# The scale and shift of every layer norm on ScalarE instead of VectorE, in a fused two-layer decoder

## The chip, the cores and the metric

The kernel runs on one core of a Trainium2 chip. The metric is device time in microseconds (us) of one execution. The core has five engines that work side by side, each on its own queue of instructions in a fixed order: TensorE (PE in the profile, with its weight loads as PEld), VectorE (DVE), ScalarE (ACT), GpSimd (POOL) and SyncE (SP, which here only issues transfers). They wait for one another with semaphores. An engine that waits holds up everything that stands behind the wait in its queue.

## The reference, cut to what matters

The input x has 16 sequences of 512 positions and 256 features. It goes through two decoder layers of three blocks each, and every block adds to x what it computes from a layer norm of x, so there are six layer norms:

```python
def _layernorm(x, axis=-1, eps=1e-05):
    m = jnp.mean(x, axis=axis, keepdims=True)
    v = jnp.var(x, axis=axis, keepdims=True)
    return (x - m) / jnp.sqrt(v + eps)
...
    x = x + _L0_attn_ref(_layernorm(x, axis=-1), ...)    # gated linear scan, with an RMS norm of its own
    x = x + _L0_xattn_ref(_layernorm(x, axis=-1), ...)   # cross attention, 16 heads, 64 keys
    x = x + _L0_ffn_ref(_layernorm(x, axis=-1), ...)     # linear with a low-rank term
    x = x + _L1_attn_ref(_layernorm(x, axis=-1), ...)    # LSTM of 20 cells that places Gaussian windows
    x = x + _L1_xattn_ref(_layernorm(x, axis=-1), ...)   # cross attention with a gate
    x = x + _L1_ffn_ref(_layernorm(x, axis=-1), ...)     # 8 experts, one chosen per row
```

All is computed in float32.

## The kernel before

**Units.** The 512 positions are cut into 4 chunks of 128 and the 16 sequences into 4 groups of 4. A unit is one chunk of one group in one layer: a tile `l_xres` of 128 partitions (positions) by 4 sequences by 256 features. There are 16 units of layer 0 and 16 of layer 1. Two units are in work at a time, in two lanes with tiles of their own (`l0_...` and `l1_...`; the profile leaves the number out). A third stream is the LSTM, which is a chain of 512 small steps over all 16 sequences.

**Stages.** Stage 0 has two loop bodies, each with two layer-0 units, one per lane. Stage 1 has two bodies, two layer-0 units and 64 LSTM steps in each. Stages 2 and 3 have four bodies each: a layer-0 unit in lane 0, a layer-1 unit in lane 1, and 32 LSTM steps. Stage 4 has four bodies with a layer-1 unit and 32 LSTM steps, and stage 5 four bodies with a layer-1 unit alone. In the trace the stages begin near 95, 230 (second body), 352, 722, 1450, 2153 and 2720 us.

**The norm.** A layer-0 unit has four norms (k = 0 to 3: before the scan, the attention, the linear block, and the one whose output feeds layer 1), a layer-1 unit two (k = 4 and 5). That makes 16 x 4 + 16 x 2 = 96 norms. One norm goes as follows. VectorE takes statistics (`bn_stats`, `bn_aggr`) of the two halves of the tile, two sequences each (step `stat`), and adds epsilon (L1034). GpSimd raises the variance to the power -1/2 (step `root`, L1332; `ln_rstd`). VectorE then makes `l_xnat`, (x - mean) x rstd, in four instructions of 128x256, two to a half (step `norm`, function `normalise`, L1050). TensorE transposes each half of `l_xnat` (step `turn`, L681), ScalarE copies both halves to `l_xT` (step `land`, L890) once the second `turn` is done, and the matmuls of the block follow. Norm k = 0 has a second root for the RMS norm (L1329), and its scale is the product of the two roots (`ln_tmp`, L1130).

**What sets the order.** Each stage body has a plan. `norm_steps`, `attention_steps`, `layer0_steps`, `layer1_steps` and `lstm_steps` list steps with an engine, an assumed cost and the steps that they need; `planned` places them one by one, by the earliest start and the longest rest of the way, and every engine's queue follows that order. Where TensorE would stand idle for long in stages 0, 4 and 5, `planned` also places matmuls on a constant (`warm`, L761) as fill. So a step that changes engine or cost changes the order of all five queues.

Other lines that the text names: L879 and L882 are the LSTM's two tanh on ScalarE, L1276, L1278, L1282 and L1288 its work on VectorE, and L753 its matmul. L1346, L1353 and L1358 are GpSimd's work in the attention, L1303 its addition of a bias row.

## Time and profile before

| | |
|---|---|
| median of 3 runs | 3200.73 us (3198.63 to 3203.84) |
| span of the profiled execution, first to last instruction | 3192.7 us |
| TensorE matmul busy | 2765.4 us (87%) |
| VectorE busy | 2130.4 us (67%) |
| ScalarE busy | 960.5 us (30%) |
| GpSimd busy | 1047.5 us (33%) |
| mean granted TensorE clock | 0.902 of full speed |

The span leaves out what comes before the first and after the last instruction; the median of the runs is 8.0 us above it. Busy shares are averages over stages that are limited by different things, so the rows further down are taken stretch by stretch: 95 to 352 us is stage 0, 352 to 722 stage 1, 722 to 2153 stages 2 and 3, and 2153 to the end stages 4 and 5.

### The profile page before, as it was taken

To read this page: it belongs to the slowest core of one execution; us is meant where nothing else is said; L and a number is where in the kernel's file an instruction comes from. 1 tells how busy PE (TensorE), PEld (TensorE's weight loads), DVE (VectorE), ACT (ScalarE), POOL (GpSimd) and SP (SyncE) were. 2 spreads that over 40 slices of the span, in tenths; PEclk is the share of its full clock that TensorE was granted. 3 is DMA by queue.
4 is the path that set the end of the run, shared out by engine and by line. 5 is a ranking of instruction groups with operands and counts; after the bars stand their busy time and mean duration, and the time that the engine had idled before them with its cause. 6 is when DMAs were issued, how large, how long until landed. Compare 5 with 4: busy or idle time off the path is not lost.

```text
span 3192.7 us, 37478 instructions
## 1 busy us (share of the span) xinstructions
PE 2765.4 (87%) x11655; PEld 1627.7 (51%) x11733; DVE 2130.4 (67%) x5978; ACT 960.5 (30%) x2361; POOL 1047.5 (33%) x956
## 2 busy tenths in 40 slices
PE   5799885976888889897988988898989899899999
PEld 2466453452545545464645555564555445555555
DVE  3576786877778687867778686866475655534434
ACT  0133242332323333332323233332222232222222
POOL 0264332233424242523425242513141321413422
PEclk9899996987898889888889898898989898999999
DMA  4210101011010100101010101001011010110100
GB/s 171 62 53 10 61 11 37 1 51 33 15 50 14 51 14 20 37 25 46 25 46 14 57 14 37 14 29 32 21 40 33 14 33 14 40 53 14 53 27 7
DMA packets 127163, 110.35 MB, mean 35 GB/s; under 512 B 31234, under 2 KB 126039, under 8 KB 126624
## 3 DMA queue, kind: packets, MB, share of 16 engines
q1 hardware_dynamic: 127008, 108.55, 11.0%
q8 instruction: 64, 1.05, 0.1%
q14 instruction: 91, 0.75, 0.1%
HBM read 76.81 MB, written 31.72 MB: 34 GB/s over the span
## 4 chain that ended last, share of the span: by engine, by line
PE 37%; issue 27%; DVE 24%; POOL 7%; ACT 2%; SPq 1%; DMA 1%; DVEq 0%; POOLq 0%; ACTq 0%
PE p L781 5%; PE p L687 4%; PE p L842 4%; PE p L720 4%; PE p L744 3%; PE p L854 3%; DVE l_xnat L1050 3%; DVE uprod L1276 3%; PE p L681 2%; PE p L698 2%; DVE l_scratch L1076 2%; PE pg L753 2%; DVE gates L1278 2%; PE p L734 2%; POOL l_scratch L1358 2%
## 5 line engine op out<-in xcount | busy, mean ns | idle before, releaser
L1346 POOL TENSOR_TENSOR l_kbd<-l_kg,headmask 128x512 f32<-128x512 f32 x256 | 265.5, 1047 | 388.4 <-PE p L720 289.7
L1332 POOL TENSOR_TENSOR ln_rstd<-ln_ve,neghalf 128x4 f32<-128x4 f32 x96 | 98.2, 1023 | 893.8 <-DVE ln_ve L1034 893.2
L744 PEld LDWEIGHTS p<-l_vg,l_scratch 128*128 128x128 f32 x2048 | 286.8, 215 | 122.0 <-DVE l_xnat L1093 64.7
L1353 POOL TENSOR_TENSOR l_scratch<-l_scratch,l_mx 128x512 f32<-128x512 f32 x256 | 266.9, 1046 | 200.0 <-DVE l_mx L1080 199.3
L744 PE MATMUL p<-l_vg,l_scratch 128*128 128x34 f32 x2048 | 297.2, 296 | 40.5 <-DVE l_xnat L1093 32.8
L720 PE MATMUL p<-l_kbd,l_qT 128*128 128x512 f32 x512 | 294.4, 666 | 40.9 <-DVE l_scratch L1076 40.9
L1276 DVE SCALAR_TENSOR_TENSOR uprod<-gates 16x40 f32<-16x40 f32 x512 | 187.0, 365 | 213.0 <-ACT gates L879 210.5
L879 ACT ACTIVATE gates<-pg 16x80 f32<-16x80 f32 x512 | 114.8, 224 | 700.8 <-PE pg L753 699.8
L761 PE MATMUL p<-warm 128*128 128x512 bf16 x1009 | 278.3, 399 | 5.9 <-issue 3.6
L842 PE MATMUL p<-l_xT,wfc 128*128 128x512 f32 x512 | 278.9, 637 | 1.1 <-DVE hr L1233 1.0
L681 PE MATMUL p<-ident,l_xnat 128*128 128x128 f32 x1024 | 195.2, 325 | 90.7 <-DVE l_xnat L1050 89.1
L854 PE MATMUL p<-wpj,hq 128*128 128x256 f32 x1024 | 264.9, 387 | 8.3 <-ACT hq L955 8.3
L753 PE MATMUL pg<-wcat,slots 128*16 128x80 f32 x1024 | 172.9, 255 | 112.3 <-DVE slots L1288 110.1
L753 PEld LDWEIGHTS pg<-wcat,slots 128*16 128x16 f32 x1024 | 58.4, 97 | 357.4 <-DVE slots L1288 193.2
L882 ACT ACTIVATE tcell<-gates 16x20 f32<-16x20 f32 x512 | 110.4, 216 | 432.1 <-DVE gates L1278 431.6
L854 PEld LDWEIGHTS p<-wpj,hq 128*128 128x128 f32 x1024 | 187.0, 190 | 90.9 <-issue 59.2
L681 PEld LDWEIGHTS p<-ident,l_xnat 128*128 128x128 f32 x1024 | 141.0, 167 | 168.9 <-DVE l_xnat L1050 131.5
L1076 DVE TENSOR_TENSOR l_scratch<-p,l_neg 128x512 f32<-128x512 f32 x256 | 174.2, 682 | 55.7 <-PE p L720 50.4
L734 PE MATMUL p<-ident,l_scratch 128*128 128x128 f32 x1024 | 181.4, 309 | 18.3 <-DVE l_xnat L1093 8.6
L908 ACT ACTIVATE l_scratch<-p 128x512 f32<-128x512 f32 x256 | 149.1, 589 | 146.6 <-PE p L734 145.9
L1278 DVE SCALAR_TENSOR_TENSOR gates<-uprod 16x20 f32<-16x20 f32 x512 | 175.2, 342 | 17.6
L1282 DVE SCALAR_TENSOR_TENSOR hnew<-gates,tcell 16x20 f32<-16x20 f32 x512 | 137.8, 269 | 73.1 <-ACT tcell L882 72.3
(165 smaller groups left out, 4764.6 us busy)
## 6 DMA issues: line engine op xcount, KB each, us to landing
xln<-xln_dram SPq DMA_DIRECT2D x40, 512.0 KB, 4.4
l_vg<-v_dram SPq DMA_DIRECT2D x32, 544.0 KB, 3.9
l_kg<-k_dram SPq DMA_DIRECT2D x32, 256.0 KB, 4.2
xln_dram<-l_xnat SPq DMA_DIRECT2D x16, 512.0 KB, 3.0
x_dram<-l_xres SPq DMA_DIRECT2D x16, 512.0 KB, 4.1
l_xres<-x_dram SPq DMA_DIRECT2D x16, 512.0 KB, 3.6
out<-l_xres SPq DMA_DIRECT2D x16, 512.0 KB, 2.9
xin<-in_x SPq DMA_DIRECT2D x12, 512.0 KB, 3.8
```

Source lines behind the costliest of these rows:

```text
L681: i = pe.transpose(banks[l][m][:, b * P:(b + 1) * P], src[:, b, m * P:(m + 1) * P], ident[:, :])
L720: pe.matmul(banks[l][j], w.qT[:, j, b * P:(b + 1) * P], w.kbd[b % 2][:, j, :, :].rearrange("p a k -> p (a k)"), start=True, stop=True).the ...
L734: i = pe.transpose(t_bank[l][:, p * P:(p + 1) * P], src, ident[:, :])
L744: i = pe.matmul(o_bank[l][:, q * VW:(q + 1) * VW], w.exT[:, j, p, :], w.vg[:, b, q * VW:(q + 1) * VW], start=True, stop=True)
L753: pe.matmul(pg[0:B, 0:80], slots[:, s % STEPS, :], wcat[:, :], start=True, stop=True).then_inc(l_pe, 1)
L761: pe.matmul(pg[:, :] if layer == 0 else banks[0][0], warm[:, 0:P], warm[:, :], start=True, stop=True)
L842: i = pe.matmul(banks[1][2 + i_ % 2], wfc[:, k, i_ * P:(i_ + 1) * P], tiles[1].xT[:, k, :], start=(k == 0), stop=(k == NH - 1))
L854: i = pe.matmul(pairs[1][:, b * D:(b + 1) * D], hq[i_ % 2][:, b * P:(b + 1) * P], wpj[:, i_, :], start=(i_ == 0 and b % 2 == 0), stop=(i_ ...
L1276: dve.scalar_tensor_tensor(uprod[:, :], gates[:, 0:40], 1.0, gates[:, 60:100], ALU.add, ALU.mult).then_inc(l_u, 1)
L1278: dve.scalar_tensor_tensor(gates[:, 80:100], uprod[:, 20:40], 0.5, uprod[:, 0:20], ALU.mult, ALU.add).then_inc(l_c, 1)
L1346: pool.tensor_tensor(w.kbd[b % 2][:, j, :, :], w.kg[:, j, b:b + 1, :].broadcast_to([P, NE, SK]), headmask[:, :].rearrange("p (a o) -> p a ...
L1353: pool.tensor_tensor(ex, ex, w.mx[:, i_ % 4, :].rearrange("p (a o) -> p a o", o=1).broadcast_to([P, NE, SK]), ALU.subtract).then_inc(t.shi ...
```

## The change

The step `norm` becomes two steps. A new VectorE step `offset` makes `shift` = -mean x scale for the four sequences at once, one instruction of 128x4. Then `norm` runs on ScalarE: four activations of the identity function, 128x256 each, with `scale` and `shift` as operands that hold one value per partition. The waits that stood ahead of the old step (for the root; for k = 0 also for the store of the former `l_xnat` and for its `turn`) are split between the two. A new wait on GpSimd keeps the first root of a layer-0 unit from overwriting `rstd` while the ScalarE still reads it for the unit before. In `norm_steps` the costs are 0.2 (0.4 for k = 0) for `offset` and 0.8 for each half of `norm`, where 0.65 stood.

```diff
--- before.py
+++ after.py
@@ -75,7 +75,9 @@
         self.stats, self.mv = sb(f"{name}_stats", [P, GB, 6]), sb(f"{name}_mv", [P, GB, 2])
         self.ve, self.rstd = sb(f"{name}_ve", [P, 2, GB]), sb(f"{name}_rstd", [P, 2, GB])
         self.tmp = sb(f"{name}_tmp", [P, 4, GB])
+        self.shift = sb(f"{name}_shift", [P, GB])
         self.small, self.inv, self.normed = sem(f"{name}_small"), sem(f"{name}_inv"), sem(f"{name}_normed")
+        self.offset = sem(f"{name}_offset")
         self.turned, self.landed = sem(f"{name}_turned"), sem(f"{name}_landed")
 
     def before(self, layer, n, k):
@@ -152,7 +154,8 @@
     steps += [("pool", "root", k, 1.0, [("stat", 2 * k + 1)])]
     if rms:
         steps += [("dve", "rms", 0, 0.6, [("root", k)]), ("pool", "root", 9, 1.0, [("rms", 0)])]
-    steps += [("dve", "norm", 2 * k + h, 0.65, [("root", 9 if rms else k)]) for h in range(2)]
+    steps += [("dve", "offset", k, 0.4 if rms else 0.2, [("root", 9 if rms else k)])]
+    steps += [("act", "norm", 2 * k + h, 0.8, [("offset", k)]) for h in range(2)]
     steps += [("pe", "turn", 2 * k + h, 0.45, [("norm", 2 * k + h)]) for h in range(2)]
     steps += [("act", "land", 2 * k + h, 0.5, [("turn", 2 * k + 1)]) for h in range(2)]
     return steps
@@ -883,7 +886,20 @@
 
             def act_step(lane, layer, family, i_, c, g, n, m):
                 t, w, l0 = at[lane], tiles[lane], scans[lane]
-                if family == "land":
+                if family == "norm":
+                    k, h = divmod(i_, 2)
+                    s = ln[lane]
+                    if h == 0:
+                        act.wait_ge(s.offset, s.before(layer, n, k) + 1)
+                        if k == 0 and positive(n):
+                            act.wait_ge(l0.xln_store, 16 * n)
+                            act.wait_ge(s.turned, 2 * s.before(0, n, 0))
+                    src, scale = (w.xres, s.rstd[:, 0, :]) if k else (xin[lane], s.tmp[:, 1, :])
+                    for b in (2 * h, 2 * h + 1):
+                        i = act.activation(w.xnat[:, b, :], src[:, b, :], ACT.Identity, bias=s.shift[:, b:b + 1],
+                                           scale=scale[:, b:b + 1])
+                    i.then_inc(s.normed, 1)
+                elif family == "land":
                     k, h = divmod(i_, 2)
                     if h == 0:
                         act.wait_ge(ln[lane].turned, 2 * ln[lane].before(layer, n, k) + 2)
@@ -1045,11 +1061,9 @@
                 dve.tensor_tensor(s.tmp[:, 2, :], s.mv[:, :, 0], s.rstd[:, 0, :], ALU.mult).then_inc(s.small, 1)
                 dve.tensor_scalar(s.tmp[:, 0, :], s.rstd[:, 0, :], 1.0, None, ALU.add).then_inc(s.small, 1)
 
-            def normalise(s, h, scale, src, dst):
-                for b in (2 * h, 2 * h + 1):
-                    i = dve.tensor_scalar(dst[:, b, :], src[:, b, :], s.mv[:, b, 0:1], scale[:, b:b + 1],
-                                          ALU.subtract, ALU.mult)
-                i.then_inc(s.normed, 1)
+            def offset(s, scale):
+
+                dve.scalar_tensor_tensor(s.shift[:, :], s.mv[:, :, 0], -1.0, scale, ALU.mult, ALU.mult).then_inc(s.offset, 1)
 
             def add_product(l, h, done):
 
@@ -1118,21 +1132,15 @@
                         statistics(s, h, small, w.xres)
                 elif family == "rms":
                     rms(s, s.before_small(0, n, 0), s.before_roots(0, n, 0))
-                elif family == "norm":
-                    k, h = divmod(i_, 2)
-                    if k:
-                        if h == 0:
-                            dve.wait_ge(s.inv, s.before_roots(layer, n, k) + 1)
-                        normalise(s, h, s.rstd[:, 0, :], w.xres, w.xnat)
+                elif family == "offset":
+                    if i_:
+                        dve.wait_ge(s.inv, s.before_roots(layer, n, i_) + 1)
+                        offset(s, s.rstd[:, 0, :])
                         return
-                    if h == 0:
-                        dve.wait_ge(s.inv, s.before_roots(0, n, 0) + 2)
-                        dve.tensor_tensor(s.tmp[:, 1, :], s.rstd[:, 0, :], s.rstd[:, 1, :], ALU.mult).then_inc(s.small, 1)
-                        if positive(n):
-                            dve.wait_ge(l0.xln_store, 16 * n)
-                            dve.wait_ge(s.turned, 2 * s.before(0, n, 0))
-                        dve.wait_ge(s.small, s.before_small(0, n, 0) + 11)
-                    normalise(s, h, s.tmp[:, 1, :], xin[lane], w.xnat)
+                    dve.wait_ge(s.inv, s.before_roots(0, n, 0) + 2)
+                    dve.tensor_tensor(s.tmp[:, 1, :], s.rstd[:, 0, :], s.rstd[:, 1, :], ALU.mult).then_inc(s.small, 1)
+                    dve.wait_ge(s.small, s.before_small(0, n, 0) + 11)
+                    offset(s, s.tmp[:, 1, :])
                 elif family == "base":
                     if i_ == 0:
                         if positive(n):
@@ -1328,6 +1336,8 @@
                         pool.wait_ge(s.small, s.before_small(0, n, 0) + 8)
                         pool.tensor_tensor(s.rstd[:, 1, :], s.ve[:, 1, :], neghalf[:, :], ALU.pow).then_inc(s.inv, 1)
                     else:
+                        if i_ == 0 and positive(n):
+                            pool.wait_ge(s.normed, 2 * s.before(0, n, 0))
                         pool.wait_ge(s.small, s.before_small(layer, n, i_) + 5)
                         pool.tensor_tensor(s.rstd[:, 0, :], s.ve[:, 0, :], neghalf[:, :], ALU.pow).then_inc(s.inv, 1)
                 elif family == "brow":
```

The plans come out in another order. Three places follow, in the names of the instructions: `l1_` and `ln1_` are tiles of lane 1, `p1` its PSUM banks.

VectorE, stage 5, loop body, around the first norm (k = 4). Before:

```order
L1251 TENSOR_SCALAR l1_scratch<-p1 1x512
L1252 ISA
L1253 TENSOR_TENSOR l1_scratch<-l1_scratch,jrow 1x512
L1254 REGISTER_ALU
L1255 TENSOR_TENSOR l1_scratch<-l1_scratch 1x4x128
L1125 REGISTER_ALU
L1050 TENSOR_SCALAR l1_xnat<-l1_xres,ln1_mv,ln1_rstd 128x256 x4
L1257 REGISTER_ALU
L1258 SCALAR_TENSOR_TENSOR l1_scratch<-l1_scratch 1x516
L1261 TENSOR_SCALAR l1_scratch<-l1_scratch 1x512
```

And now:

```order
L1259 TENSOR_SCALAR l1_scratch<-p1 1x512
L1260 ISA
L1261 TENSOR_TENSOR l1_scratch<-l1_scratch,jrow 1x512
L1262 REGISTER_ALU
L1263 TENSOR_TENSOR l1_scratch<-l1_scratch 1x4x128
L1137 REGISTER_ALU
L1066 SCALAR_TENSOR_TENSOR ln1_shift<-ln1_mv,ln1_rstd 128x4
L1265 REGISTER_ALU
L1266 SCALAR_TENSOR_TENSOR l1_scratch<-l1_scratch 1x516
L1269 TENSOR_SCALAR l1_scratch<-l1_scratch 1x512
```

The four instructions of the norm are gone from the middle of the `rows` work (the 1x512 instructions, for the next unit), and one of 128x4 stands in their place.

ScalarE, stage 5, loop body, around the second norm (k = 5), which follows the end of the attention. Before:

```order
L908 ACTIVATE l1_scratch<-p1 128x512 x3
L894 ACTIVATE l1_xT<-p1 128x512 x2
L889 ISA
L890 ACTIVATE l1_xT<-p1 128x512 x2
```

And now:

```order
L924 ACTIVATE l1_scratch<-p1 128x512 x4
L910 ACTIVATE l1_xT<-p1 128x512 x2
L893 REGISTER_ALU
L899 ACTIVATE l1_xnat<-l1_xres,ln1_shift,ln1_rstd 128x256 x4
L905 ISA
L906 ACTIVATE l1_xT<-p1 128x512 x2
```

Four activations now stand between the last copy of the attention (`l1_xT` by L894, L910 in the changed file) and the copy after the `turn` (L890, now L906).

ScalarE, stage 3, loop body, at the norm k = 0 of lane 0 between LSTM steps. Before:

```order
L879 ACTIVATE gates<-pg 16x80
L882 ACTIVATE tcell<-gates 16x20
L889 ISA
L890 ACTIVATE l0_xT<-p0 128x512 x2
L878 REGISTER_ALU
L879 ACTIVATE gates<-pg 16x80
L882 ACTIVATE tcell<-gates 16x20
L930 REGISTER_ALU
L931 ACTIVATE l1_scratch<-p1 1x512
```

And now:

```order
L882 ACTIVATE gates<-pg 16x80
L885 ACTIVATE tcell<-gates 16x20
L893 ISA
L895 REGISTER_ALU
L896 REGISTER_ALU
L899 ACTIVATE l0_xnat<-xin,ln0_shift,ln0_tmp 128x256 x4
L881 REGISTER_ALU
L882 ACTIVATE gates<-pg 16x80
L905 REGISTER_ALU
L906 ACTIVATE l0_xT<-p0 128x512
L885 ACTIVATE tcell<-gates 16x20
```

Between the two tanh of one LSTM step (`tcell`) and the first tanh of the next (`gates`) stood two copies of 128x512; now four activations stand there and one copy behind the tanh.

The number of `warm` matmuls grows from 70 to 82 in each body of stage 0, from 135 to 139 (134 to 135 in the last body) in stage 4, and from 135 to 141 (133 to 136 in the last) in stage 5: 24 + 13 + 21 = 58 more in all.

## Rows read from the trace of the kernel before

**Rows 1.** Page, parts 1 and 4: busy time of the engines; the chain's shares.

```profile
PE 2765.4 (87%) x11655; PEld 1627.7 (51%) x11733; DVE 2130.4 (67%) x5978; ACT 960.5 (30%) x2361; POOL 1047.5 (33%) x956
...
PE 37%; issue 27%; DVE 24%; POOL 7%; ACT 2%; SPq 1%; DMA 1%; DVEq 0%; POOLq 0%; ACTq 0%
```

**Rows 2.** Four stretches; columns PE, PEld, DVE, ACT, POOL busy, then clock, DMA.

```profile
95.00:352.00 257.00, 238.15 (x1080) 150.98 (x1090) 174.29 (x489) 80.64 (x140) 114.59 (x98) 0.97 0.14 41
352.00:722.00 370.00, 292.53 (x1219) 164.25 (x1220) 290.63 (x987) 126.73 (x384) 119.60 (x111) 0.86 0.09 27
722.00:2153.00 1431.00, 1227.70 (x4980) 742.82 (x4979) 1090.37 (x2956) 466.65 (x1170) 516.46 (x468) 0.87 0.10 30
2153.00:3192.70 1039.70, 953.15 (x4060) 541.49 (x4126) 542.09 (x1442) 279.79 (x658) 296.67 (x276) 0.94 0.10 29
```

**Rows 3.** The chain by line, of 352 to 722 and of 722 to 2153.

```profile
by line: PE p L781 12.8%; PE p L687 10.4%; DVE uprod L1276 6.0%; PE pg L753 6.0%; PE p L720 5.3%; DVE l_xnat L1050 5.2%; DVE gates L1278 5.1%; issue 4.4%; PE p L744 4.3%; DVE hnew L1282 4.2%; PE p L698 3.4%; DVE slots L1288 3.3%; DVE ln_sta
...
by line: issue 17.1%; PE p L687 5.5%; PE p L842 4.9%; PE p L744 4.8%; PE p L854 4.7%; DVE uprod L1276 4.5%; PE p L720 4.1%; PE p L781 3.8%; DVE l_scratch L1076 3.8%; DVE l_xnat L1050 3.7%; PE p L681 3.4%; DVE l_mx L1080 2.7%; DVE gates L127
```

**Rows 4.** Line L1050 alone in the four stretches: its busy time on DVE.

```profile
95.00:352.00 257.00, 26.56 (x64) 0.97 0.14 41
352.00:722.00 370.00, 28.30 (x64) 0.86 0.09 27
722.00:2153.00 1431.00, 102.68 (x192) 0.87 0.10 30
2153.00:3192.70 1039.70, 35.32 (x64) 0.94 0.10 29
```

**Rows 5.** Waits of the turns for L1050, stretch by stretch: total, times, longest.

```profile
PE p L681 <- DVE l_xnat L1050: 19.6, 11, 13.3
...
PE p L681 <- DVE l_xnat L1050: 10.7, 8, 2.9
...
PE p L681 <- DVE l_xnat L1050: 36.0, 25, 3.7
...
PE p L681 <- DVE l_xnat L1050: 22.9, 16, 2.6
```

**Rows 6.** Groups by shape: busy us, mean ns of one; line L1050's min/median/max.

```profile
L882 ACT ACTIVATE tcell<-gates 16x20 f32<-16x20 f32 x512 | 110.4, 216 | 432.1 <-DVE gates L1278 431.6
...
L903 ACT ACTIVATE l_scratch<-l_scratch 128x512 f32<-128x512 f32 x256 | 158.4, 620 | 65.1 <-POOL l_scratch L1353 64.6
...
L908 ACT ACTIVATE l_scratch<-p 128x512 f32<-128x512 f32 x256 | 149.1, 589 | 146.6 <-PE p L734 145.9
...
L897 ACT ACTIVATE l_qT<-p,biasQ 128x512 f32<-128x512 f32 x64 | 43.3, 677 | 35.1 <-PE p L698 35.1
...
L1045 DVE TENSOR_TENSOR ln_tmp<-ln_mv,ln_rstd 128x4 f32<-128x4 f32 x16 | 2.5, 154 | 0.0
...
L1130 DVE TENSOR_TENSOR ln_tmp<-ln_rstd 128x4 f32<-128x4 f32 x16 | 11.8, 738 | 0.1
...
L1050 DVE TENSOR_SCALAR l_xnat<-l_xres,ln_mv,ln_rstd x320: 379/407/2806, 148.6 to 3147.2; 128x256 f32<-128x256 f32 x160
```

**Rows 7.** Timeline, last stage, second norm of a body: start, duration, what.

```profile
2912.16 3.34 PEld L761 LDWEIGHTS p<-warm 128*128 128x128 bf16 x16
...
2914.62 1.02 POOL L1332 TENSOR_TENSOR ln_rstd<-ln_ve,neghalf 128x4 f32<-128x4 f32 x1 [11.05 <-DVE ln_ve L1034]
...
2915.61 2.09 POOL L1346 TENSOR_TENSOR l_kbd<-l_kg,headmask 128x512 f32<-128x512 f32 x2
...
2915.67 2.82 DVE L1050 TENSOR_SCALAR l_xnat<-l_xres,ln_mv,ln_rstd 128x256 f32<-128x256 f32 x4 [1.13 <-POOL ln_rstd L1332]
...
2917.90 1.30 PE L681 MATMUL p<-ident,l_xnat 128*128 128x128 f32 x8 [1.92 <-DVE l_xnat L1050]
...
2919.24 1.09 ACT L890 ACTIVATE l_xT<-p 128x512 f32<-128x512 f32 x2 [10.48 <-PE p L681]
```

**Rows 8.** Timeline, first stage, a norm with GpSimd idle.

```profile
277.04 1.38 DVE L1050 TENSOR_SCALAR l_xnat<-l_xres,ln_mv,ln_rstd 128x256 f32<-128x256 f32 x4 [1.12 <-POOL ln_rstd L1332]
```

## Prediction

> **What bounds the kernel now.** Read the busy shares and the chain first [rows 1]: TensorE is busy for 87% of the span, VectorE for 67%, ScalarE for 30%. The chain of waits runs 37% through TensorE, 24% through VectorE and 2% through ScalarE. So the change moves work from an engine that is often on the path to one that hardly is. Then go by stretches [rows 2]. In stages 1 to 3 (352 to 722 and 722 to 2153 us) VectorE is busy for 290.6 of 370 and 1090.4 of 1431 us, 77%, beside a TensorE at 79% and 86%: two engines with in-order queues that keep each other waiting. In stage 0 (95 to 352) and in stages 4 and 5 (from 2153) TensorE is at 93% and 92%, fill included, and VectorE at 68% and 52%. There the units go through their steps one after another, and what counts of a norm is how long it takes, not which engine it takes.
>
> Of the norm itself you see two things. Line L1050 is busy for 192.9 us in all [rows 4], 2.01 us for each of 96 norms. And TensorE stands idle before a `turn` until L1050 is done for 19.6, 10.7, 36.0 and 22.9 us in the four stretches, 60 times in 192 halves [rows 5]. The first of these holds one wait of 13.3 us at the start of the program, which is no property of a norm.
>
> **What one norm costs before and after.** Four instructions of L1050 take 1.38 us with GpSimd idle [rows 8]. The mean is 2.01, since VectorE waits for GpSimd: in the last stage the four take 2.82 us while two instructions of L1346 run [rows 7], and single ones go from 379 ns to 2806 [rows 6]. The waits are 0.63 us a norm.
>
> The ScalarE form, 128x256 from SBUF with two operands per partition, is in no row. From 16x20 (216 ns) to 128x512 from SBUF (620 ns) is 0.82 ns a column, so 256 columns take 410 ns. One operand per partition adds 88 ns (L897 at 677 against L908 at 589) [rows 6]. The second adds between nothing and the same again: 498 to 586 ns. I take 586, since the only operand that a row shows costs that. Two copies in a row take 1.09 us [rows 7], 0.09 less than twice 589, so four activations take 4 x 0.586 - 3 x 0.09 = 2.07 us (1.72 at the low end), and a half 1.08. A price for this form stands in the Trainium skill, "ScalarE: Activation LUTs", What ACT_TABLE_LOAD costs: 186 ns and 0.833 ns a column, 93 ns for each such operand, 93 ns of overlap. By it the estimate for four is 2.06 us and the sum below is the same; no run here shows it yet.
>
> `offset` (128x4, two SBUF inputs) lies between L1045 at 154 ns, which never meets GpSimd, and L1130 at 738 ns, which stands right behind a root as `offset` will [rows 6]. I take 0.50 us. It inherits the wait for GpSimd that the first of the four had, as in [rows 7], but not the later ones. The Trainium skill says why, in "Advanced Engine Details and Errata", GPSIMD Details: GpSimd shares a read and a write interface with VectorE, and conflicts with instructions of two SBUF inputs, which `offset` is. By that rule the wait stays, and at most its share on three of four instructions goes; the trace agrees for L1130.
>
> From one engine's end to the next's start are 0.03 us (root end 2915.64, L1050 start 2915.67) [rows 7]. So from the root to a finished `l_xnat` are 0.50 + 0.03 + 2.07 = 2.60 us where 2.01 stood: 0.6 us longer. With GpSimd idle it is 0.15 + 0.03 + 2.07 = 2.25 for 1.38, 0.87 longer. With the cheap activation and a busy GpSimd it is 2.25 for 2.01, 0.24 longer. VectorE gets back 2.01 - 0.50 = 1.5 us a norm, 145 us in all; ScalarE takes on 96 x 2.07 = 199 us.
>
> **Stages 4 and 5.** 16 norms, one lane, nothing beside it but the LSTM. `turn` waits for the norm, `land` for both turns: 16 x 0.6 = +9.6 us (3.8 to 13.9). That VectorE comes free earlier gives nothing here, for what follows it, the `rows` work and then the first mask, waits for the norm's own successors.
>
> **Stage 0.** 16 norms in two lanes, eight pairs. Lane 1's norm is 0.6 longer. Lane 0 gains VectorE's 1.5 us and then pays 0.6. But the ScalarE order puts its norm ahead of lane 1's query copy. I take +0.6 a pair, 8 x 0.6 = +4.8 us (-4 to +7).
>
> **Stages 1 to 3.** 64 norms, 131.0 us of L1050 [rows 4]. On the chain are 5.2% of 370 and 3.7% of 1431 us [rows 3], 19.2 + 52.9 = 72 us. TensorE stood idle for 33 of the 128 halves, 26% [rows 5]; I take this share of the 72, 19 us, as norms whose length counts, and the other 53 us as norms that only stood in VectorE's queue ahead of something wanted.
> - The 53 us leave the path, but the next late thing is near: TensorE at 86% is itself an engine that others wait for. I take half, -26.5 (bounds -53 and -13).
> - 64 x 0.50 = 32 us of `offset` come in, by the same share (53/131) and half: +6.5.
> - 33 halves wait 0.6 longer, 20 us; of the 46.7 us of such waits 19 were on the chain, 40%: +8.
> - ScalarE carries 64 x 2.07 = 132 us more in 1801, 7.4% of the time. 384 LSTM steps have two tanh each on it. A tanh that comes while a half of a norm runs waits half of 1.08 us: 768 x 0.074 x 0.54 = 31 us in all. The LSTM holds about a quarter of the chain in stage 1 (L1276, L753, L1278, L1282, L1288: 24.6%) and less after [rows 3]. I take a fifth: +6 (0 to 31).
>
> Together -6 us.
>
> **The `warm` fill.** 58 more at 3.34/16 = 0.21 us [rows 7] are 12 us. They stand ahead of turns that now come later: in [rows 7] TensorE still stood idle 1.92 us behind its fill. I cost them at nothing; were this cover gone, it would be 12.
>
> **Sum.** 9.6 + 4.8 - 6 = +8.4 us on a span of 3192.7, 3201.1. The runs' median is 8.0 above the span, so 3209.
>
> **The rivals.**
> Longer norms win slightly (the sum): 3209, its own range 3201 to 3225. For it speak the 60 waits of [rows 5], against it the 77% of VectorE.
> VectorE's relief wins. The 53 us go nearly whole, because VectorE's queue, not TensorE, paces stages 1 to 3: -53 + 6.5 + 8 + 6 = -32, with stages 0, 4 and 5 at +14 is -18, so 3183. With the cheap activation and `offset` at 0.15 the terms are -53 + 2 + 3 + 6 and +4, -38, so 3163. For it: VectorE is at 77% there, and its lines hold much of the chain [rows 3]. Against it: 2 us of a norm that end one wait on VectorE begin one on ScalarE.
> ScalarE's queue becomes the wait, the case of the other sign. The order puts four activations in one block ahead of the next LSTM tanh, where two copies stood. If the tanh waits for them each time on the path, the 31 us count in full and the relief shrinks to a quarter: -13 + 6.5 + 20 + 31 = +44, with +14 is 3259. From about half of the 31 us on the path on, it outweighs the relief. The Trainium skill speaks for it, in "ScalarE: Activation LUTs", Rules for kernel authors: adding and multiplying belong on VectorE. The rows say 407 ns there against my estimate of 586.
> Nothing moves: gain and loss cancel within 6 us, 3201. So would it be if the new order hid both.
>
> **How the numbers follow.** Longer norms 0.40, relief 0.33, ScalarE's queue 0.15, nothing 0.12. The predicted time is 3209. The range 3163 to 3250 reaches to the low end of the relief and most of the way to 3259; the likeliest case alone is 3201 to 3225. 0.2%, 6.4 us, is about what a measurement tells from no change. Slower by more: most of the first case and the third, 0.45. Within: the last and a part of the first, 0.20. Faster: 0.35.
>
> **What would show it.** Right: ScalarE near 1160 us busy and VectorE near 1985; activations of 0.58 us; `offset` near 0.5; waits of L681 now for ScalarE, longer by about 0.6 each; stages 4 and 5 longer by some 10 us, stages 1 to 3 within 10 of before. Wrong: stages 1 to 3 shorter by 25 us or more with TensorE's waits for L1288 and L1076 well down (relief), or LSTM waits on ScalarE grown by tens of us (queue). A lower TensorE clock than 0.86 to 0.87 in stages 1 to 3 [rows 2] would be a cost that I left out.

## Result: the time and the profile after

The changed kernel takes 3210.91 us, median of 6 runs (3207.78 to 3217.0), beside 3199.72 us for the kernel before (6 runs, the three of the table included, 3196.95 to 3205.56): a ratio of 1.0033, 95% interval 1.002 to 1.0046. It is slower by 0.33%, 11 us. The forecast was 3209. The ratios of the experiments further down stand against executions of the kernel before made beside each of them (medians 3197.36 to 3201.37), and come from all runs, so they can differ by 0.1% from a quotient of medians.

The page of the changed kernel, parts 1 and 4, to be read beside [rows 1]. The last digits of each entry are shares and instruction counts.

```profile
PE 2803.7 (87%) x11791; PEld 1647.6 (51%) x11791; DVE 1990.3 (62%) x5690; ACT 1149.6 (36%) x2745; POOL 1045.9 (33%) x956
...
issue 34%; PE 32%; DVE 18%; POOL 10%; ACT 4%; SPq 1%; DMA 1%; POOLq 0%; DVEq 0%; ACTq 0%
```

VectorE lost 140 us of work, ScalarE gained 189, and the chain runs less through VectorE (18% for 24%). The time went up all the same.

The norm's new instructions: first the groups of lines L899 and L1066 with min/median/max in ns, then the groups by shape with busy us and mean ns.

```profile
L899 ACT ACTIVATE l_xnat<-l_xres,ln_shift,ln_rstd x320: 582/585/601, 147.8 to 3160.6; 128x256 f32<-128x256 f32 x160
...
L1066 DVE SCALAR_TENSOR_TENSOR ln_shift<-ln_mv,ln_rstd x80: 128/164/2673, 147.7 to 3158.9; 128x4 f32<-128x4 f32 x80
```

```profile
L1066 DVE SCALAR_TENSOR_TENSOR ln_shift<-ln_mv,ln_rstd 128x4 f32<-128x4 f32 x80 | 43.7, 546 | 20.8 <-POOL ln_rstd L1342 19.0
...
L1066 DVE SCALAR_TENSOR_TENSOR ln_shift<-ln_mv,ln_tmp 128x4 f32<-128x4 f32 x16 | 19.3, 1206 | 0.6
```

The activation of 128x256 takes 582 to 602 ns wherever it stands (of its other two groups, with the scale of k = 0, the longest is 602). `offset` takes 164 ns at the median of the 80 in the first group, and 0.66 us on average over all (63.0 us for 96), because it stands right behind a root, when GpSimd goes on to its next work. The timeline of the last stage shows the norm that answers to [rows 7]:

```profile
2929.59 1.02 POOL L1342 TENSOR_TENSOR ln_rstd<-ln_ve,neghalf 128x4 f32<-128x4 f32 x1 [11.37 <-DVE ln_ve L1050]
2930.58 2.04 POOL L1356 TENSOR_TENSOR l_kbd<-l_kg,headmask 128x512 f32<-128x512 f32 x2
2930.64 1.00 DVE L1066 SCALAR_TENSOR_TENSOR ln_shift<-ln_mv,ln_rstd 128x4 f32<-128x4 f32 x1 [1.13 <-POOL ln_rstd L1342]
2931.67 2.08 ACT L899 ACTIVATE l_xnat<-l_xres,ln_shift,ln_rstd 128x256 f32<-128x256 f32 x4 [7.95 <-DVE ln_shift L1066]
```

From the root's end (2930.61) to the finished `l_xnat` (2933.75) are 3.14 us, where [rows 7] had 2.85 (2915.64 to 2918.49): this norm is 0.3 us longer, not 0.6. Now by stages. The cuts lie where a stage's first layer-1 input is loaded, and at the fourth store of `x3_dram` (`x_dram` in the profile) for the end of stage 0; all stage times of this document are taken from one profiled execution of each kernel in this way. Columns as in [rows 2]; the changed kernel, stages 0 to 5:

```profile
0.00:351.40 351.40, 293.28 (x1422) 179.01 (x1423) 187.72 (x547) 118.09 (x210) 113.73 (x100) 0.98 0.23 75
351.40:727.20 375.80, 303.17 (x1228) 171.00 (x1227) 268.91 (x935) 159.14 (x448) 119.64 (x112) 0.83 0.09 27
727.20:1429.60 702.40, 605.20 (x2469) 363.38 (x2467) 505.86 (x1428) 282.47 (x689) 258.14 (x234) 0.87 0.11 32
1429.60:2159.30 729.70, 636.16 (x2520) 391.75 (x2520) 505.45 (x1397) 279.24 (x680) 259.36 (x238) 0.86 0.10 29
2159.30:2734.90 575.60, 516.35 (x2168) 285.49 (x2168) 337.84 (x965) 174.99 (x484) 150.40 (x144) 0.90 0.09 26
2734.90:3205.90 471.00, 449.52 (x1989) 256.93 (x1989) 184.51 (x422) 135.63 (x235) 144.58 (x130) 0.99 0.11 32
```

The same windows of the kernel before, stages 1 to 3:

```profile
347.30:719.60 372.30, 294.33 (x1227) 164.55 (x1226) 290.09 (x985) 127.07 (x383) 120.09 (x112) 0.86 0.09 28
719.60:1452.30 732.70, 615.78 (x2470) 370.97 (x2468) 559.49 (x1499) 236.60 (x594) 257.03 (x233) 0.85 0.10 30
1452.30:2156.70 704.40, 615.98 (x2520) 373.25 (x2520) 534.31 (x1471) 232.96 (x585) 260.90 (x239) 0.88 0.10 30
```

Against before (347.3, 372.3, 732.7, 704.4, 566.3 and 469.6 us) the six stages moved by +4.1, +3.5, **-30.3**, **+25.3**, +9.3 and +1.4 us. The span grew by 13.2 us, but that is a small rest of two large movements: stage 2 shortened by 30 and stage 3 lengthened by 25, with the same kinds of work in both. The prediction had no such terms by stage. The experiments are about them.

### The profile page after: what moved, and what is told of

Read it like the earlier page. It is cut to its first block, busy times and chain, and to the rows that moved or that the text cites. A ratio compares the mean times of both kernels' runs of the same rounds, so it can differ in the third digit from the quotient of the medians.

```text
span 3205.9 us, 37829 instructions
## 1 busy us (share of the span) xinstructions
PE 2803.7 (87%) x11791; PEld 1647.6 (51%) x11791; DVE 1990.3 (62%) x5690; ACT 1149.6 (36%) x2745; POOL 1045.9 (33%) x956
## 4 chain that ended last, share of the span: by engine, by line
issue 34%; PE 32%; DVE 18%; POOL 10%; ACT 4%; SPq 1%; DMA 1%; POOLq 0%; DVEq 0%; ACTq 0%
PE p L747 4%; PE p L784 4%; PE p L723 3%; PE p L690 3%; PE p L845 3%; PE p L857 2%; POOL l_kbd L1356 2%; PE p L737 2%; PE p L684 2%; DVE uprod L1284 2%; PE p L701 2%; POOL l_scratch L1363 2%; ACT l_xnat L899 2%; PE pg L756 2%; DVE l_scratch L1090 2%
## 5 line engine op out<-in xcount | busy, mean ns | idle before, releaser
L1356 POOL TENSOR_TENSOR l_kbd<-l_kg,headmask 128x512 f32<-128x512 f32 x256 | 266.0, 1049 | 320.7 <-PE p L723 222.0
L747 PEld LDWEIGHTS p<-l_vg,l_scratch 128*128 128x128 f32 x2048 | 298.3, 222 | 126.8 <-DVE l_xnat L1107 54.5
L747 PE MATMUL p<-l_vg,l_scratch 128*128 128x34 f32 x2048 | 308.5, 303 | 48.3 <-DVE l_xnat L1107 31.0
L1284 DVE SCALAR_TENSOR_TENSOR uprod<-gates 16x40 f32<-16x40 f32 x512 | 168.0, 328 | 284.4 <-ACT gates L882 281.1
L723 PE MATMUL p<-l_kbd,l_qT 128*128 128x512 f32 x512 | 294.0, 665 | 39.7 <-DVE l_scratch L1090 37.9
L764 PE MATMUL p<-warm 128*128 128x512 bf16 x1111 | 298.6, 398 | 0.0
L756 PE MATMUL pg<-wcat,slots 128*16 128x80 f32 x1024 | 173.8, 256 | 104.3 <-DVE slots L1296 100.1
L684 PE MATMUL p<-ident,l_xnat 128*128 128x128 f32 x1024 | 188.5, 318 | 80.9 <-ACT l_xnat L899 77.1
L899 ACT ACTIVATE l_xnat<-l_xres,ln_shift,ln_rstd 128x256 f32<-128x256 f32 x320 | 168.7, 587 | 129.0 <-DVE ln_shift L1066 128.8
L1290 DVE SCALAR_TENSOR_TENSOR hnew<-gates,tcell 16x20 f32<-16x20 f32 x512 | 162.5, 317 | 78.5 <-ACT tcell L885 77.4
```

Source lines behind the costliest of these rows:

```text
L684: i = pe.transpose(banks[l][m][:, b * P:(b + 1) * P], src[:, b, m * P:(m + 1) * P], ident[:, :])
L723: pe.matmul(banks[l][j], w.qT[:, j, b * P:(b + 1) * P], w.kbd[b % 2][:, j, :, :].rearrange("p a k -> p (a k)"), start=True, stop=True).the ...
L747: i = pe.matmul(o_bank[l][:, q * VW:(q + 1) * VW], w.exT[:, j, p, :], w.vg[:, b, q * VW:(q + 1) * VW], start=True, stop=True)
L756: pe.matmul(pg[0:B, 0:80], slots[:, s % STEPS, :], wcat[:, :], start=True, stop=True).then_inc(l_pe, 1)
L764: pe.matmul(pg[:, :] if layer == 0 else banks[0][0], warm[:, 0:P], warm[:, :], start=True, stop=True)
L899: i = act.activation(w.xnat[:, b, :], src[:, b, :], ACT.Identity, bias=s.shift[:, b:b + 1], scale=scale[:, b:b + 1])
```

## Experiments: is it the engine or the order?

The change does two things. It puts the norm on another engine, and, since the planner sees another cost and another engine, it puts the steps of all engines in another order. **Theory A (engine)**: stage times move because VectorE is relieved and ScalarE loaded. **Theory B (order)**: they move because each stage has a new order, whatever engine holds the norm. I call an order a draw where a small change of the planner's numbers picks another one, better or worse, with no rule in sight. In the kernels with a held order the planner works as in one kernel, and the norm is issued as in the other, with the waits that go with its engine.

**The engine alone.** Planner and fill as before; only when the plan is emitted does the norm go to ScalarE, and `offset` stands where the first half stood on VectorE.

```
+        if key[1] == "norm":
+            kept += [("dve", key[0], "offset", key[2] // 2)] if key[2] % 2 == 0 else []
+            who = "act"
         kept.append((who, *key))
```

> The norm on ScalarE, but every queue in the order of the kernel before: the four activations and the offset stand in the global order exactly where the four VectorE instructions stood, and the fill is that of before. In the changed kernel stages 2 and 3 (from the first load of the layer-1 input at 719.6 us to the fifth at 1452.4, and to the ninth at 2156.7) took 702 and 730 us, where 733 and 704 stood. Theory A, the engine does it: stage 2 near 705, stage 3 near 728 here too, total near 3211. Theory B, the new order does it: both stages within 8 us of before (725 to 741 and 696 to 712), with the longer norms adding 3 to 5 in stage 0 and 9 to 13 in stages 4 and 5, total 3205 to 3218 by another road.

3264.99 us, ratio 1.0218 (1.0197 to 1.0239). By stages +7.3, +15.1, +25.8, +0.7, +4.6, +10.9, together +64.3. Neither theory had this: A expected 3211 and a shorter stage 2, B at most 3218 with stage 2 within 8 us of before.

**The order alone.** Planned as the changed kernel, with its fill, but the four instructions of the norm are issued on VectorE, where the plan has `offset`.

```
-        kept.append((who, *key))
+        if key[1] == "offset":
+            kept += [("dve", key[0], "norm", 2 * key[2] + h) for h in range(2)]
+        elif key[1] != "norm":
+            kept.append((who, *key))
```

> The other half: the norm stays on VectorE, its four instructions stand where the changed kernel has its offset, and every queue and the fill are in the order of the changed kernel. Theory A (engine): stages as before, 733 and 704 us, total 3195 to 3205, plus at most a few us for an order made for other costs. Theory B (order): stage 2 near 705 and stage 3 near 728, stages 0, 4 and 5 as before, total 3190 to 3202. If both the order and the engine are needed for the gain of stage 2, it is above 725 here and in the run with the old order.

3233.65 us, ratio 1.0113 (1.0096 to 1.0129). By stages +7.9, +17.2, **-25.7**, **+29.0**, +13.6, -3.6, together +38.2. The norm never left VectorE here, and the two large movements are there. So these two movements belong to the order: B for stages 2 and 3. The total, 3234, lies some 30 us above what either theory allowed, since stages 1, 0 and 4, expected to stay as before, are 17.2, 7.9 and 13.6 longer too. And the engine is not nothing. At the new order the changed kernel is 25.0 us faster than this one (by stages -3.8, -13.7, -4.6, -3.7, -4.2, +5.0), and at the old order the same step to ScalarE costs 64.3. The two effects don't add: each engine is the worse one in the order that was planned for the other.

What it meets in stage 2 at the old order is seen in the waits of the LSTM: VectorE idle until ScalarE's tanh over the gates is done (total us, times, longest). The kernel before, the engine alone, the order alone, and both, in stage 2:

```profile
DVE uprod L1276 <- ACT gates L879: 46.7, 36, 3.4
```

```profile
DVE uprod L1286 <- ACT gates L884: 82.0, 50, 5.3
```

```profile
DVE uprod L1280 <- ACT gates L883: 37.0, 37, 3.1
```

```profile
DVE uprod L1284 <- ACT gates L882: 53.8, 47, 5.1
```

At the old order the engine adds 35 us of these waits in one stage, at the new order 17. How such a wait comes about stands in the timeline of the changed kernel, stage 4:

```profile
2266.93 2.55 DVE L1066 SCALAR_TENSOR_TENSOR ln_shift<-ln_mv,ln_rstd 128x4 f32<-128x4 f32 x1 [0.25 <-POOL ln_rstd L1342]
...
2267.31 0.31 PE L756 MATMUL pg<-wcat,slots 128*16 128x80 f32 x2
2267.42 2.04 POOL L1356 TENSOR_TENSOR l_kbd<-l_kg,headmask 128x512 f32<-128x512 f32 x2
2269.51 1.09 ACT L899 ACTIVATE l_xnat<-l_xres,ln_shift,ln_rstd 128x256 f32<-128x256 f32 x2 [3.27 <-DVE ln_shift L1066]
2270.51 0.21 ACT L882 ACTIVATE gates<-pg 16x80 f32<-16x80 f32 x1
```

The gates' product is done at 2267.62. ScalarE is idle, but its next instruction is the norm, which waits for `offset`; `offset` takes 2.55 us instead of 0.16, and ends at 2269.48, 0.02 us after GpSimd's two products of L1356; then half a norm runs, and the tanh starts 2.9 us late. Nearly two of the 2.9 us are the norm's waiting, and one is its running. Over the whole program 24 tanh over the gates of the changed kernel stood directly behind a norm whose end came later than their product, by 25.1 us in all; with the engine alone it is 35 and 29.9. The second tanh of an LSTM step (`tcell`) is held in the same way behind the instruction of VectorE that it needs: 26 times for 11.0 us in the changed kernel, 25 times for 40.6 us with the engine alone. (All four are worked out from the trace's records of ScalarE, of the products and of that instruction.) VectorE's waits for it, with the engine alone, beside 72.3 us in 192 waits in the kernel before:

```profile
DVE hnew L1292 <- ACT tcell L887: 112.9, 228, 2.3
```

Of the 40.6 us, 31.5 lie in stage 3, and stage 3 is only 0.7 us longer than before. So a tanh that is held need not cost anything; how much of it counts differs from stage to stage.

**More orders, same work.** If B holds, a change of the planner's numbers alone must move the stages as much. In the kernel before, the planned cost of half a norm is set from 0.65 to 0.60 and to 0.70. Besides the order only the fill moves, by a few matmuls a body in stages 0, 4 and 5 (stage 0: 67 and 77, where 70 stood); stages 1 to 3 have none.

```
-    steps += [("dve", "norm", 2 * k + h, 0.65, ...
+    steps += [("dve", "norm", 2 * k + h, 0.60, ...      (and 0.70)
```

> The kernel before, its instructions all kept; only the planner's cost of half a norm is 0.60 instead of 0.65, which moves a few steps of the orders of stages 1 to 3 (4 to 150 places of some 570 in single stages). Theory order (the -30 us of stage 2 and the +25 us of stage 3 in the changed kernel are properties of the orders, each of which is a draw with a spread of some 20 us a stage, whatever norm they hold): stages 2 and 3 move by 10 to 30 us each in either direction, total anywhere from 3160 to 3240. Theory engine (the stage times move because a norm takes no VectorE time): nothing moves a stage by more than 5 us here, total 3194 to 3206.

3229.87 us, ratio 1.0105 (1.0082 to 1.0129). Stages +0.6, +8.6, -8.8, +35.4, -5.8, -0.6.

> As the one with 0.60, with the planner's cost of half a norm at 0.70. Theory order: again stages move by 10 to 30 us, and not in the opposite direction of the 0.60 kernel stage by stage, since the orders are draws and no slope: total 3160 to 3240. Theory engine: 3194 to 3206 and no stage moved by over 5 us.

3208.12 us, ratio 1.0022 (1.0008 to 1.0035). Stages +4.7, -0.4, -11.8, +23.9, +2.2, -3.7.

A twentieth of a microsecond in a number that no instruction carries makes the kernel 1% slower (0.60), three times as much as the whole change under study. B holds, and these are no steps along a slope: 0.60 and 0.70 both make stage 2 shorter and stage 3 longer. Part of how an order costs time can be read off. Stage 3 with 0.60:

```profile
1452.70:2192.50 739.80, 636.31 (x2520) 392.56 (x2520) 545.85 (x1471) 236.35 (x585) 261.55 (x239) 0.86 0.10 29
```

Against stage 3 of before (above) it has the same 2520 matmuls, but they hold TensorE for 636.3 us instead of 616.0: 20 of the 35 us. The granted clock is 0.86 for 0.88. One group of stage 3, before and with 0.60:

```profile
L744 PE MATMUL p<-l_vg,l_scratch 128*128 128x34 f32 x512 | 73.2, 294 | 6.0 <-DVE l_xnat L1093 6.0
```

```profile
L744 PE MATMUL p<-l_vg,l_scratch 128*128 128x34 f32 x512 | 85.4, 321 | 14.5 <-DVE l_xnat L1093 9.2 <-ACT l_scratch L908 5.1
```

The same 512 products take 12 us more, and wait 8.5 us more ahead of them. The changed kernel shows the same in its stage 3: 636.2 us of matmuls at 0.86, 20 of its 25 us. Busy time here can hold stalls within a group as well as a lower clock, so I don't split the 20 us further. Nor is it all a property of the order. The same stage in the changed kernel's order, first with the norm on VectorE, then on ScalarE with the extra instructions of a later experiment:

```profile
1451.70:2185.10 733.40, 628.22 (x2520) 385.45 (x2520) 528.26 (x1468) 232.35 (x584) 258.95 (x236) 0.88 0.10 29
1459.60:2194.90 735.30, 625.97 (x2520) 383.27 (x2520) 505.13 (x1397) 300.94 (x728) 259.45 (x238) 0.88 0.10 29
```

Both have the clock of before, 0.88, and hold TensorE for 12 and 10 us more than before, in stages that are 29 and 31 us longer. So some 10 to 12 us come with the order at an unchanged clock; the other 8 to 10, with the 0.86, were not there in every kernel of this order.

**One stage at a time.** The norm on ScalarE, with the changed kernel's order, in one stage alone; all other stages in code and order as before.

```
+ON_ACT = (2,)       (and (3,))
+    on = stage in ON_ACT      handed to norm_steps, which takes the old or the new steps
```

> The norm on ScalarE in stage 2 alone, with the changed kernel's plan there, and on VectorE with the plan of before in the other stages. The changed kernel won 30 us in stage 2 and lost in all others. If stages stand for themselves: 3200 - 30 = 3170 (3166 to 3176). Rival, what stage 2 wins is handed on as a later wait in stage 3 (which lost 25 us in the changed kernel): stage 2 near 703 again but stage 3 above 720, total near 3195.

3170.95 us, ratio 0.9918 (0.9901 to 0.9934). Stages +0.2, +1.5, **-24.0**, -2.2, +3.4, -3.0: the gain of stage 2 comes back alone, and this kernel is 0.8% faster than before and 1.2% faster than the changed one.

> Scale and shift on ScalarE in stage 3 alone (its 16 norms and its order from the changed kernel), every other stage as before. If the +25.4 us of stage 3 belong to its order and engine there, they come back here: stage 3 +25 (20 to 30), the rest within 5, total 3225. If they were handed down by stage 2, which in the changed kernel ends 30 us earlier (late work pushed over the boundary), stage 3 stays within 8 us of before and the total at 3205.

3218.79 us (3214.61 to 3233.7), ratio 1.0057 (1.0037 to 1.0077). Stages +2.1, +5.2, +1.2, **+28.0**, +2.7, +0.1. The loss of stage 3 comes back alone too, so it isn't handed down by an early stage 2. But the profiled execution is the slowest of this kernel's six, 15 us above the median, at a granted clock of 0.890 where the four fastest have 0.894 or 0.895. The median is 18.7 us above before, so in a usual execution the loss of stage 3 is likely nearer to 19 than to 28 us.

These two and the composite further down also say how far one profile of a stage can be trusted: stages whose code was as before came out between 3.0 us shorter and 5.6 us longer. Stage movements under 6 us are not told apart from nothing by one profile. Where one stage has one order in two kernels but not the same stages ahead of it, it can differ by more: stage 2 took 702.4 us in the changed kernel and 708.7 here.

**The planner's costs made true.** The changed kernel with half a norm planned at 1.08 (the measured length) instead of 0.8, and `offset` at 0.5 (0.8 in the first norm) instead of 0.2 (0.4). And again its order with the norm on VectorE.

```
-    ("dve", "offset", k, 0.4 if rms else 0.2, ...   ("act", "norm", 2 * k + h, 0.8, ...
+    ("dve", "offset", k, 0.8 if rms else 0.5, ...   ("act", "norm", 2 * k + h, 1.08, ...
```

> The changed kernel with the planner's costs set to what was measured: half a norm on ScalarE 1.08 instead of 0.8, offset 0.5 (0.8 in the first norm of a chunk) instead of 0.2 (0.4). Instructions the same but for the warm fill. Theory order: the planner's numbers pick the order, and an order from true costs is one more draw, 3180 to 3240, with stages 1 to 3 moved by 10 us or more each. Theory that the wrong costs (a half that really takes 1.08 planned at 0.8) made tanh steps queue behind the norms: the LSTM's waits for ScalarE's gates fall from 281 towards the 210 us of before, and stages 1 to 3 get shorter by 15 us or more together, 3180 to 3195.

3182.22 us, ratio 0.9948 (0.993 to 0.9966). Stages +6.4, +2.3, -26.7, +7.1, -2.9, +0.1. 29 us faster than the changed kernel with the same instructions but for the fill (97 in each body of stage 0, where the changed kernel has 82). The reason that I had for it fell: the LSTM's waits for the gates hardly moved. Whole span, the changed kernel and this one:

```profile
DVE uprod L1284 <- ACT gates L882: 281.1, 220, 6.7
```

```profile
DVE uprod L1284 <- ACT gates L882: 284.0, 219, 7.5
```

> The orders and the warm fill of the kernel with true costs, but with the norm's four instructions back on VectorE, where offset stands there. It gives the effect of the engine at a third fixed order. The engine is worth -25 us at the changed kernel's order and +64 at the old one. If the orders are draws and an engine fits the order that was planned for it, ScalarE should again be the better one here: this kernel 3182 + 15 to 40, 3197 to 3222, its stage 3 near that of true costs (711 us, an order's property) and its stages 0, 4 and 5 within 8 us of it. If the engine's effect were one number, it would come out near the mean of the two, -20: 3162.

3215.21 us, ratio 1.0057 (1.004 to 1.0074). By stages against the ScalarE one: +1.0, +11.3, +3.3, +25.2, +0.2, -2.8, so the engine is worth -38.2 us here. That ScalarE is the better one at an order planned for it came back, near the upper end of what was expected. That stage 3 would stay at 711 did not: it went to 736.7, so "a stage's time is a property of its order" is too strong; it is one of order and engine together.

What this doesn't show is that the norm is better off on ScalarE. The two kernels with a held order have the norm on an engine that the planner had not counted on. Where each engine has orders planned for it, the spans against before are 0, +29.3 and +14.7 us for VectorE (planned at 0.65, 0.60 and 0.70) and +13.2, -13.9 and, with the split that follows, +49.6 for ScalarE. These two sets overlap, so which engine is better isn't settled here.

**Splitting the norm in the queue.** To take the blocked tanh away by itself, the planner may place each of the four activations alone.

```
-    ("act", "norm", 2 * k + h, 1.08, [("offset", k)]) for h in range(2)
+    ("act", "norm", 4 * k + b, 0.54, [("offset", k)]) for b in range(4)
```

> As true costs, but the planner may place each of the four ScalarE instructions of a norm by itself (0.54 each) instead of in blocks of two, so that an LSTM tanh can slip between. Same instructions. If the LSTM's waits behind whole halves are what ScalarE's norm costs (281 us against 210), the waits of uprod for ScalarE's gates fall by 20 us or more and stages 1 to 3 get shorter by some 10: 3165 to 3175. If the order is a mere draw, the waits may fall and the time still go anywhere between 3170 and 3225; I expect this, near 3185.

3236.71 us, ratio 1.0119 (1.0096 to 1.0141). Stages +15.0, +15.0, +0.9, +23.0, -6.7, +2.6. The waits did what was intended, over the whole span:

```profile
DVE uprod L1284 <- ACT gates L882: 257.7, 218, 8.2
```

26 us less than with true costs, and the tanh directly behind a norm now lose 14.0 us instead of 18.6 over the gates, and 9.8 instead of 19.2 at `tcell`. In stage 4, 6.8 of the 14.0 are still there: `offset` waits for GpSimd as before, and the tanh still stands behind the first of the four activations. The time went up by 54 us. The new order took back far more than the removed wait had cost, and 3236.7 lies above the range that I had written. (The fill grew too, to 113 in each body of stage 0, and that stage is 8.6 us longer than with true costs; the two were not taken apart.) It shows how little an experiment by way of this planner says of the one wait it was meant to test.

**The price of a microsecond on each engine**, at a fixed order: here nothing is planned anew. One more instruction of the norm's kind in each half, into a tile that nothing reads: 192 more activations in the changed kernel, and 192 more of the VectorE form in the kernel with the order alone.

```
+ act.activation(spare[lane][:, h, :], src[:, 2 * h, :], ACT.Identity, bias=..., scale=...)
+ dve.tensor_scalar(s.spare[:, h, :], src[:, 2 * h, :], ..., ALU.subtract, ALU.mult)      (the other kernel)
```

> The changed kernel with one more activation of 128x256 in each half of a norm, into a tile that nothing reads: a norm is 1.0 us longer (0.5 at its first half) and ScalarE has 192 x 0.5 = 96 us more. By the prediction's terms a longer norm counts in full in stages 4 and 5 (16 x 1.0 = +16), once a pair in stage 0 (+8), and in stages 1 to 3 at 33 of 128 halves by 40%, with as much again for LSTM steps that wait (+10 to +20): total +34 to +44 over the changed kernel's 3211, 3245 to 3255. Rival, ScalarE has room in stages 1 to 3: +24 alone, 3235. Rival, ScalarE's queue paces stages 1 to 3: +60 or more, over 3270.

3266.22 us, ratio 1.0214 (1.0197 to 1.0231), 55 us above the changed kernel, 11 more than the most that I had expected and 4 less than the rival of a queue that paces the stages. By stages +7.0, +6.4, +16.6, +5.6, +6.6, +13.9.

> The kernel with the changed orders and the norm on VectorE (3234 us), with one extra 128x256 instruction of the norm's kind on VectorE in each half, into a tile that nothing reads: 192 more, some 0.45 to 0.5 us each, about 90 us of VectorE time and as much length. Its counterpart, the same doubling on ScalarE in the changed kernel, put in 96 us and cost 56, 0.58 us for each. If a microsecond of VectorE costs no more than one of ScalarE (what counts is only the norm's length), this costs 52 us: 3286. If VectorE's time is worth more, which would explain why at this same order the engine move gained 25 us although it adds 54 us more to ScalarE than it takes from VectorE, it costs about 0.95 for each, 85 us: 3319. The line between them is 3303.

3300.13 us, ratio 1.0306 (1.0289 to 1.0323); its span is 64.1 us above the kernel with the order alone, by stages +9.4, +8.1, +20.5, +16.3, +3.6, +6.2. The sums over stages 1 to 3, for the changed kernel and the ScalarE doubling:

```profile
sum 1807.90, PE 1544.53 PEld 926.13 DVE 1280.22 ACT 720.85 POOL 637.14; mean PE 514.84 PEld 308.71 DVE 426.74 ACT 240.28 POOL 212.38
```

```profile
sum 1836.50, PE 1531.90 PEld 913.71 DVE 1280.82 ACT 778.06 POOL 637.35; mean PE 510.63 PEld 304.57 DVE 426.94 ACT 259.35 POOL 212.45
```

57.2 us more of ScalarE cost 28.6 us: 0.50 each. In stages 0, 4 and 5 30.7 us cost 27.5: 0.90 each, nearly all of it, as it should be where the units go one after another. For VectorE the same sums, for the order alone and the VectorE doubling:

```profile
sum 1829.90, PE 1533.61 PEld 918.11 DVE 1349.90 ACT 596.85 POOL 638.32; mean PE 511.20 PEld 306.04 DVE 449.97 ACT 198.95 POOL 212.77
```

```profile
sum 1874.80, PE 1550.22 PEld 923.72 DVE 1389.00 ACT 594.94 POOL 637.73; mean PE 516.74 PEld 307.91 DVE 463.00 ACT 198.31 POOL 212.58
```

39.1 us more of VectorE cost 44.9 us: 1.15 each, and in stages 0, 4 and 5 20.4 us cost 19.2: 0.94. In all 59.5 us cost 64.1, 1.08 each, where ScalarE has 0.64 (56.1 for 87.9). The line that I had drawn between the two theories was 3303, and 3300 is just on the side of equal prices. But it was drawn for 90 us of added VectorE time, and only 59.5 came. By instruction the two doublings cost about the same, 0.33 and 0.29 us; by microsecond VectorE's time was the dearer, twice as dear in the contended stages. It is one profile each, at an order planned without the norm on VectorE, and the orders' draws can't be ruled out of such a difference even here, where queues shift against each other.

Do these prices explain what the engine was worth at this order? An estimate from them: in stages 1 to 3 the move takes 69.7 us from VectorE and gives ScalarE 124.0, -80 + 62 = -18 us, and -21.9 was measured. In stages 0, 4 and 5 it would be -38 + 58 = +20, and -3.1 was measured. So they fit where the queues contend and miss where they don't.

**A composite.** Stage 2 as in the changed kernel, stage 4 as planned with 0.60, stage 5 as planned with 0.70, the rest as before.

```
+    on, NORM = stage in ON_ACT, {4: 0.6, 5: 0.7}.get(stage, 0.65)
```

> Put together from stages: stage 2 as in the changed kernel (ScalarE), stage 4 in the order planned with a norm at 0.60, stage 5 in the order planned with 0.70, stages 0, 1 and 3 as before. If a stage's time is a property of its own order, the parts add: 0 + 0 - 24 + 0 - 5.8 - 3.7, 3160 (3155 to 3168). If a stage's time depends on how the stage ahead ends, or the single profiles' gains in stages 4 and 5 were noise, it stays at 3171.

3171.53 us, ratio 0.992 (0.9901 to 0.994). Stages +0.3, +5.6, -24.0, -2.2, +3.3, -3.8. No better than stage 2 alone: the 5.8 us that stage 4 gained in the profile with 0.60 did not come back. The same order of stage 4 took 560.5 us there and 569.6 here, so the gain was scatter or hung on how stage 3 ends; this run doesn't tell which. Stage 2 in the changed kernel's order is shorter for the third time (30.3, 24.0 and 24.0 us).

## Why the prediction was near, and what in it was wrong

All kernels that separate order and engine, spans of the profiled executions against 3192.7:

| order | norm on VectorE | norm on ScalarE | ScalarE minus VectorE |
|---|---|---|---|
| before | 0 | +64.3 | +64.3 |
| changed kernel | +38.2 | +13.2 | -25.0 |
| true costs | +24.3 | -13.9 | -38.2 |
| norm at 0.60 | +29.3 | not run | |
| norm at 0.70 | +14.7 | not run | |

By the medians of the runs, each against the executions of before beside it, the VectorE column is +34.7, +17.8, +29.7 and +8.0 for the four new orders, and the last column +66.0, -23.5 and -35.8: the same signs.

- **The prices of the instructions: right.** 585 ns for an estimate of 586, four in 2.08 us for 2.07, ScalarE at 1149.6 us for 1160, VectorE at 1990.3 for 1985. The Trainium skill, "ScalarE: Activation LUTs", What ACT_TABLE_LOAD costs, gives 2.06 us for the four by the estimate in the prediction; the trace agrees within 0.02.
- **`offset` at 0.50: too low**, 0.66 on average; 15 us more over 96. Its wait for GpSimd stayed, as the Trainium skill has it in "Advanced Engine Details and Errata", GPSIMD Details; the trace agrees with 164 ns at the median and 2.55 us beside L1356.
- **Stages 4 and 5, +9.6: the sum right (+10.7), the reason half right.** In stage 5, where nearly no step changes place, the engine cost +5.0, +2.8 and +10.9 us at the three orders, for a term of 8 x 0.6 = 4.8. In stage 4 it was worth -4.2, -0.2 and +4.6, and the order cost +13.6 at VectorE. What I said of stage 4, that VectorE's relief gives nothing beside the LSTM and only length counts, is not what these show, though most of them lie within the 6 us scatter.
- **Stage 0, +4.8: +4.1 measured**, made of +7.9 by the order and -3.8 by the engine. Again the sum and not the working, as far as movements within the scatter of 6 us say anything.
- **Stages 1 to 3, -6: -1.5 measured**, by +3.5, -30.3 and +25.3. **This is the step that failed.** Its terms were all terms of the engine (-26.5 + 6.5 + 8 + 6). At the changed kernel's order the engine gave -21.9 there (-13.7, -4.6, -3.7), 16 us better than my sum. The order, which I costed at nothing outside stage 0, gave +20.5 (17.2 - 25.7 + 29.0). The two errors nearly cancelled, and that was luck. Taken the other way round, the engine first, it is +41.5 (15.1 + 25.8 + 0.7) for the engine at the old order and -43 for the new order with the norm on ScalarE: neither has one value by itself, and a sum without a term for the order could not have either.
- **"33 halves wait 0.6 longer": right at a held order, wrong in the sum.** The turns' waits over the whole span, for ScalarE now, against 89.1 us in 60 waits before [rows 5], and below it the order alone, with the norm on VectorE:

```profile
PE p L684 <- ACT l_xnat L899: 77.1, 62, 13.6
```

```profile
PE p L685 <- DVE l_xnat L1054: 62.9, 39, 12.6
```

Against before they didn't grow. Against the same order with the norm on VectorE they grew by 14.2 us, at true costs by 8.9 (43.7 to 52.6), at the old order by 21.2 (89.1 to 110.3). The longer norm does what I said of it; the orders planned for ScalarE take it back, since the norm lies elsewhere in them.
- **ScalarE's queue at 31 us in all: the direct blocking was 36.1** (25.1 over the gates, 11.0 at `tcell`), of the size that I said, but in part by another way: I counted the time that half a norm runs, and the longest of these waits, near 3 us, have the tanh behind a norm that waits for `offset`, and `offset` for GpSimd. The sign of being wrong that I had named, LSTM waits on ScalarE grown by tens of us, did appear: 281.1 us for the gates (above), where the kernel before and the order alone have

```profile
DVE uprod L1276 <- ACT gates L879: 210.5, 200, 5.9
```

```profile
DVE uprod L1280 <- ACT gates L883: 242.5, 196, 6.0
```

32 of the 71 us came with the order and 39 with the engine. Not all of it need be delay, for a VectorE with less work also gets to this wait earlier. At the old order this rival's time came true: 3265 us, close to its 3259, with +41.5 us in stages 1 to 3 for its +44. There the direct blocking is 70.5 us, but nearly half of it lies in stage 3, which was only 0.7 us longer, so the nearness is in part luck.
- **The relief rival** needed "stages 1 to 3 shorter by 25 us or more". Stage 2 alone shows 30, but the order alone has 26 of them with the norm still on VectorE. The engine's part at the new order, -21.9, lies 10 us from this rival's -32 and 16 from the -6 that I took: at this order half of the 53 us was too little relief, at the old order the engine's part has the other sign, +41.5. The waits that this rival named moved little: TensorE's for the LSTM (`slots`, L1288) from 110.1 to 100.1 us, for the mask (L1076) from 40.9 to 37.9.
- **The fill at nothing**: not tested apart from the order. The kernel with the order alone has the 58 more, and its stage 5 was 3.6 us shorter, so nothing speaks against it there.
- **The clock**: the prediction named a clock below 0.86 in stages 1 to 3 as a cost left out. It fell to 0.83 in stage 1 (0.86 before) and to 0.86 in stage 3 (0.88), and matmuls there took 9 and 20 us more. Of the 20, some 10 to 12 come with the order, at a clock of 0.88, as shown above. The 9 are no effect of the change that I can show: with the norm moved in stage 3 alone, stage 1 is in code and order that of before and has them too.

```profile
349.40:726.90 377.50, 302.10 (x1227) 168.60 (x1225) 290.24 (x985) 126.98 (x383) 120.05 (x112) 0.83 0.09 27
```

So 3209 for 3211 is right, but as a sum of parts that were partly wrong: the total hid a draw of the order that can be 38 us by itself, in either direction stage by stage. Over the whole program all four new orders with the norm on VectorE were slower than the one of before. What stays open is why an order is good. In the kernels whose stage 3 is 24 to 35 us longer, matmuls that hold TensorE longer account for 10 to 22 of them; what in the order sets this off, and where the rest lies, was not found.

## What to carry to other kernels

Where a planner sets the order, a change of a step's engine or cost is two changes: measure the one with the order held and the order with the engine held before believing either, and give the order its own term with a spread from a few runs with the costs shifted slightly (here 15 to 38 us on 3200 in the profiled executions, 8 to 35 by medians). Then the stages that gained can be kept and the others left as they were: here one of six gave 0.8%, where the change everywhere lost 0.3%.

A step moved to an in-order queue blocks it while it waits, not only while it runs; look at what the moved step's own input waits for. How much of the blocking shows in the time is another question: with 31.5 us of it one stage here was 0.7 us longer.
